# Tile loads that transpose 16-bit halves, and fifteen result tiles combined on TensorE inside the tile loop

## What is computed

```python
h = layernorm(x).reshape(-1, 256)                 # 2048 tokens
scores = sigmoid(h @ gate_w.T); sc = scores + gate_bias
# the best 4 of 8 groups, in them the best 8 of 32 experts, weights normalised, times 2.5
combine = (one_hot(tki, 32) * tkw[..., None]).sum(1)
g = silu(einsum('th,eih->tei', h, w_gate)); u = einsum('th,eih->tei', h, w_up)   # i = 128
routed = einsum('tei,ehi->th', g * u * combine[:, :, None], w_down)
shared = silu(h @ sh_gate.T) * (h @ sh_up.T) @ sh_down.T
return x + routed + shared
```

## Time and profile before

| | |
|---|---|
| median of 3 runs | 613.6 us |
| the profiled execution | 612.29 us, of which span 611.0 us |
| PE busy | 563.9 us (92%) |
| DVE busy | 407.4 us (67%) |
| ACT busy | 372.3 us (61%) |
| POOL busy | 361.8 us (59%) |
| granted clock of PE, mean | 0.976 |
| DMA | 119.69 MB, mean 196 GB/s |

### The profile page before, as it was taken

The page is one execution under the profiler, slowest core; times in us unless marked ns, Lnnn a source line. Parts: engine busy times, 40 slices in busy tenths (PEclk is TensorE's granted clock), DMA queues, the critical chain, the costliest instruction groups (busy, mean ns, idle before and its releaser), DMA issues.

```text
span 611.0 us, 11524 instructions
## 1 busy us (share of the span) xinstructions
PE 563.9 (92%) x2677; PEld 422.3 (69%) x2677; DVE 407.4 (67%) x1554; ACT 372.3 (61%) x993; POOL 361.8 (59%) x414
## 2 busy tenths in 40 slices
PE   3989989889999798798997999999999999999996
PEld 2666557655766455555666888888788888888875
DVE  6975675986768987647776444444444444688897
ACT  1867888868786755552611666566566666677760
POOL 4343233632143377876777777777777777777730
PEclk9979999999999899899799999999999999999999
DMA  8999300000000023239364999876666666999966
GB/s 258 394 397 383 131 0 2 1 1 0 2 0 0 17 92 119 98 119 343 119 222 167 304 321 342 293 223 214 200 202 205 209 207 198 346 412 407 411 255 222
DMA packets 62063, 119.69 MB, mean 196 GB/s; under 512 B 8667, under 2 KB 45583, under 8 KB 59951
## 3 DMA queue, kind: packets, MB, share of 16 engines
q1 hardware_dynamic: 48079, 77.63, 37.5%
q0 software_dynamic: 13488, 41.04, 17.7%
q10 hardware_dynamic: 432, 0.29, 0.3%
HBM read 61.29 MB, written 57.64 MB: 195 GB/s over the span
## 4 chain that ended last, share of the span: by engine, by line
PE 78%; DVE 10%; ACT 6%; DMA 3%; issue 1%; POOL 1%; SPq 0%; DVEq 0%; POOLq 0%; ACTq 0%
PE ps L2023 22%; PE ps L2043 11%; PE ps L1671 7%; PE ps L1656 6%; PE ps L1882 5%; PE ps L1682 5%; PE ps L1695 5%; PE ps L2036 3%; PE ps L1642 3%; PE ps L1777 3%; PE ps L1783 2%; DVE tokrow L750 2%; PE ps L1794 2%; DMA arena<-yrows 2%; DMA xs<-in_x 1%
## 5 line engine op out<-in xcount | busy, mean ns | idle before, releaser
L2023 PE MATMUL ps<-arena,mats 128*128 x636 | 164.0, 381 | 0.3 <-issue 0.3
L609 POOL DMA_INDIRECT xrows<-tokrow,place_of x128 | 125.2, 978 | 41.8 <-issue 37.5
L1267 DVE TENSOR_TENSOR mats<-ps,mats 128x128 f32<-128x128 f32 x159 | 46.3, 291 | 106.1 <-ACT mats L1453 101.1
L2023 PEld LDWEIGHTS ps<-arena,mats 128*128 128x128 f32 x636 | 108.6, 191 | 8.8 <-issue 0.5
L2043 PE MATMUL ps<-arena,mats 128*128 x318 | 95.5, 383 | 1.0 <-DVE mats L1274 1.0
L1453 ACT ACTIVATE mats<-ps 128x128 f32<-128x128 f32 x159 | 44.1, 277 | 56.4 <-PE ps L2023 56.4
L1446 ACT COPY mats<-ps 128x256 f32<-128x256 f32 x159 | 58.0, 365 | 11.9 <-PE ps L1882 11.9
L1387 ACT ACTIVATE hat<-tokrow,total 128x256 f32<-128x256 f32 x96 | 47.6, 499 | 18.8 <-DVE tokrow L815 11.7
L1395 ACT ACTIVATE hat<-tokrow,shift,rstd 128x256 f32<-128x256 f32 x96 | 49.7, 591 | 12.9 <-POOL shift L540 12.8
L2043 PEld LDWEIGHTS ps<-arena,mats 128*128 128x128 f32 x318 | 48.0, 191 | 13.7 <-issue 2.1
L545 POOL TENSOR_SCALAR var_eps<-variance 128x4 f32<-128x4 f32 x24 | 6.4, 269 | 83.5 <-ACT hat L1387 83.2
(11 more groups left out here) (237 smaller groups left out, 1136.0 us busy)
## 6 DMA issues: line engine op xcount, KB each, us to landing
hat<-xrows SPq DMA_DIRECT2D x81, 160.0 KB
rows<-xrows SPq DMA_DIRECT2D x78, 160.0 KB
arena<-in_experts SPq DMA_DIRECT2D x4, 1920.0 KB, 18.8
xrows<-padrow SPq DMA_DIRECT2D x32, 160.0 KB
hat<-yrows SPq DMA_DIRECT2D x5, 1024.0 KB, 8.4
tokrow<-yrows SPq DMA_DIRECT2D x5, 1024.0 KB
hatT<-yrows SPq DMA_DIRECT2D x5, 1024.0 KB, 8.9
xrows<-padrow SPq DMA_DIRECT2D x1, 4960.0 KB
```

Source lines behind the costliest of these rows:

```text
L609: gp.indirect_dma_start(out=xrows[:, :], out_offset=bass.IndirectOffsetOnAxis(ap=place_of[:, g, k:k + 1], axis=0), in_=tokrow[:, g, :], in ...
L2023: mm = te.matmul(bank(6 + u)[:, 0:2 * I], turned_row[u][:, dc * P:(dc + 1) * P], arena[:, dc * D:(E - 1) * WCOL + (dc + 1) * D][:, bass.ds ...
```

## The change

1. **Transposing loads.** `turn_row` is gone. The row buffer is filled by two DMAs on SP's queue: `dma_start_transpose` of the 256 channels seen as 512 16-bit halves, and a plain load of the 64 columns of weights and destinations. Its source needs the low halves and the high halves of a row apart, so ACT's new `halve(i)` writes them so into `slots`, one copy of 2048 halves per partition for each block; `normalise(i, 6)` now writes into `hat`, and POOL's `dispatch` waits for `halved` in place of `normed`. `copy_row` on ACT puts the halves together again: 512 halves per partition from SBUF in place of 256 floats from PSUM.
2. **Fifteen kept tiles.** KEPT is 15, tiles 144 to 158. Their four matmuls each stand inside the tile loop on PE, five iterations behind the tile's own; POOL scatters 144 tiles instead of 153. The 0/1 matrices go round six buffers. Two token tiles share a PSUM bank.
3. **Order.** ASK_AT, SUM_AT and SHIFT_AT are new; only six loads of results are asked for inside SP's loop. `ask_back(3)` waits for 112 scattered tiles. The last load of results has no buffer of its own any more and waits for sum 12 like the others.

```diff
+HALF = mybir.dt.uint16
-KEPT = 6
+KEPT = 15
+TOKEN_SETS = 6
-SHIFT_AT = 116
+SHIFT_AT = 135
-ASK_AT = [128, 129, 133, 136, 139, 142, 145, 148, 152, 155, 158]
-SUM_AT = [120, 123, 126, 129, 132, 135, 138, 141, 145, 148, 151, 154]
+ASK_AT = [140, 141, 149, 156, 157, 158]
+SUM_AT = [133, 136, 142, 148, 149, 150, 152, 153, 155, 156, 157, 158]
...
+                if g == 3:
+                    wait_scattered(-(-(YFIRST + YBUFS + 20) // YGROUP) * YGROUP)
                 if g == EARLY_SUMS:
                     wait_scattered(TILES - KEPT)
-                if g == EARLY_SUMS + 3:
-
-                    sy.wait_ge(down_done, TILES)
-                    sy.dma_start(last_back, results[g]).then_inc(row_in[0], 16)
-                    return
                 if g >= 3:
                     sy.wait_ge(out_ready, g - 2)
...
                 if n >= ROWBUFS:
-                    sy.wait_ge(row_turned, n - ROWBUFS + 1)
+                    sy.wait_ge(row_copied, n - ROWBUFS + 1)
                     sy.wait_ge(own_ready, (n - ROWBUFS) // GROUP + 1)
-                sy.dma_start(rowbuf[n % ROWBUFS], xrows[bass.ds(at[n % 4], P), :]).then_inc(row_in[n % ROWBUFS], 16)
+                sy.dma_start_transpose(rowhalf[n % ROWBUFS], halves[bass.ds(at[n % 4], P), 0:2 * D]
+                                       ).then_inc(row_in[n % ROWBUFS], 16)
+                sy.dma_start(rowbuf[n % ROWBUFS][:, WTS:ROW], xrows[bass.ds(at[n % 4], P), WTS:ROW]
+                             ).then_inc(row_in[n % ROWBUFS], 16)
...
+            def halve(i):
+                ac.wait_ge(normed[i // Q], past(i, 2 * ROUNDS, TQ))
+                ac.copy(slots[:, set_of(i), :].bitcast(HALF).rearrange("p t (h d) -> p t h d", h=2),
+                        hat[:, set_of(i), :].bitcast(HALF).rearrange("p t (d h) -> p t h d", h=2)).then_inc(halved, 1)
...
             def copy_row(s):
                 u = s % 2
-                ac.wait_ge(row_turned, s + 1)
+                ac.wait_ge(row_in[s % ROWBUFS], 32 * (s // ROWBUFS + 1))
                 if s >= 2:
                     ac.wait_ge(gate_up_done, s - 1)
-                ac.copy(turned_row[u], bank(4 + u)[:, 0:D]).then_inc(row_copied, 1)
+                ac.copy(turned_row[u].bitcast(HALF).rearrange("p (n h) -> p h n", h=2),
+                        rowhalf[s % ROWBUFS].rearrange("p (h c) r -> p h (c r)", h=2)).then_inc(row_copied, 1)
...
+            def combine(k):
+                n = TILES - KEPT + k
+                te.wait_ge(token_known, k + 1)
+                te.wait_ge(y_ready, n + 1)
+                for t in range(TQ):
+                    mm = te.matmul(bank(4 + t // 2)[:, t % 2 * D:(t % 2 + 1) * D], of_token[k % TOKEN_SETS][:, t, :],
+                                   ybuf[y_place(n)], start=k == 0 and t % 2 == 0, stop=k == KEPT - 1 and t % 2 == 1)
+                mm.then_inc(combined, 1)
...
-            for n in range(TILES + 3):
-                if 1 <= n < TILES:
-                    turn_row(n)
+            for n in range(TILES + 5):
...
-                if n >= 3:
+                if 3 <= n <= TILES + 2:
                     down(n - 3, at[n - 3])
...
+                if TILES - KEPT + 5 <= n:
+                    combine(n - 5 - (TILES - KEPT))
```

More of the change, by code:

```diff
@@ L251, in build @@
         picked = part(mats[:, 4, :, :], GROUP * E, GROUP * 2, E)
+        halves, whole_rows = xrows.bitcast(HALF), xrows.bitcast(I32)
+        rowhalf = [buf[:, 0:D].bitcast(HALF).rearrange("p (c r) -> p c r", c=2 * DC) for buf in rowbuf]
         rowgroup = [part((hat, rows)[i // 2][:, :, :], i % 2 * GROUP * ROW, GROUP, ROW) for i in range(ROWBUFS // GROUP)]
@@ L255, in build @@
             "p (k d) -> p k d", k=TOPK), hatT[0].rearrange("p c (k d) -> p (c k) d", d=D)]
-        last_back = place(arena, 0, TOPK, D)
         of_token = [part(hatT[1][:, :, :], k * TQ * P, TQ, P) for k in range(4)]
-        of_token += [part(tokrow[:, :, :], k * TQ * P, TQ, P) for k in range(KEPT - 4)]
+        of_token += [part(tokrow[:, :, :], k * TQ * P, TQ, P) for k in range(TOKEN_SETS - 4)]
         into_token = part(mats[:, 4, :, :], GROUP * E * 3, GROUP)
@@ L312, in build @@
         row_in = [sem(f"row_in{i}") for i in range(ROWBUFS)]
[L313 removed]
+        halved, row_copied, gate_up_done, silu_done = sem("halved"), sem("row_copied"), sem("gate_up"), sem("silu_done")
         matched, picked_ready, own_ready = sem("matched"), sem("picked"), sem("own")
@@ L502, in sync_program @@
                 ask_back(g)
+                if g == T and T >= len(ASK_AT):
+                    store(0, TQ)
                 if g == EARLY_SUMS - 1:
@@ L1467, in copy_out @@
                     u = y_last(n) // YGROUP
-                    ac.wait_ge(scattered[u % YGROUPS], 16 * YGROUP * (u // YGROUPS + 1))
+                    ac.wait_ge(scattered[u % YGROUPS],
+                               16 * sum(m // YGROUP % YGROUPS == u % YGROUPS for m in range(min(YGROUP * (u + 1), TILES - KEPT))))
                 ac.wait_ge(own_ready, n // GROUP + 1)
@@ L1579, in scalar_program @@
             score_tokens(0)
+            halve(0)
             evacuate(3, 3)
@@ L1589, in scalar_program @@
             score_tokens(1)
+            halve(1)
             normalise(3, 4, slots)
@@ L1607, in scalar_program @@
             score_tokens(2)
+            halve(2)
             normalise(3, 2 * ROUNDS, xs)
@@ L1611, in scalar_program @@
             score_tokens(3)
+            halve(3)
             shared_silu(2, 1)
@@ L1871, in transpose_slots @@
                 transpose_block(i, n, hat)
-            def turn_row(s):
-                u = s % 2
-                te.wait_ge(row_in[s % ROWBUFS], 16 * (s // ROWBUFS + 1))
-                if s < 2:
-                    te.wait_ge(tables_ready, 3 * (s + 2))
-                if s >= 2:
-                    te.wait_ge(row_copied, s - 1)
-                for dc in range(DC):
-                    tr = te.transpose(bank(4 + u)[:, dc * P:(dc + 1) * P], rowbuf[s % ROWBUFS][:, dc * P:(dc + 1) * P],
-                                      ident[:, :])
-                tr.then_inc(row_turned, 1)
             turn_context()
@@ L2012, in tensor_program @@
             sum_runs(2)
-            turn_row(0)
             spread_runs(2)
@@ L2063, in tensor_program @@
                     turn_act(n - 2)
-                if n >= 3:
+                if 3 <= n <= TILES + 2:
                     down(n - 3, at[n - 3])
-            te.wait_ge(row_copied, TILES)
-            te.wait_ge(act_ready, TILES)
-            for k in range(KEPT):
-                n = TILES - KEPT + k
-                te.wait_ge(token_known, k + 1)
-                te.wait_ge(y_ready, n + 1)
-                for t in range(TQ):
-                    mm = te.matmul(bank(4 + t)[:, 0:D], of_token[k][:, t, :], ybuf[y_place(n)], start=k == 0,
-                                   stop=k == KEPT - 1)
-            mm.then_inc(combined, 1)
+                if TILES - KEPT + 5 <= n:
+                    combine(n - 5 - (TILES - KEPT))
         sync_program()
```

56 lines of the change are left out of this document (26 added, 30 removed).

## The result

| | before | after |
|---|---|---|
| median | 613.9 us (612.8 to 616.1, 4 runs) | 748.9 us (745.4 to 752.0, 4 runs) |
| span of the profiled execution | 611.0 us | 746.8 us |
| ratio | | 1.219, 95% interval 1.213 to 1.226 |

The change makes the kernel 22% slower. The forecast was 626 us with a range of 604 to 646: the sign was right, the size was wrong by 123 us, and the rival that came true ("the loads set the pace") had a chance of 0.13, of which only 0.03 for a pace over 2 us.

The account below looks back on a forecast made before the run. PE and POOL's queue were taken to bound the kernel together. Late PE and DVE work ends at 619.9; 1.6 for POOL's delay and 2 for clock give a 623.5 us span, 12.5 above 611.0: 626 us, range 604 to 646.

Parts of the forecast that it names:

- the loads set the pace: Rival on SP's queue: a tile's two loads become the bound, 645 us at 1.7 us a tile; chance 0.13.
- The transposing load: SP's two loads a tile: 1.2 us to issue if alike plain ones; engines' time 0.42 to 2.8 us.
- q: Time of a tile's two loads on SP, taken as under 1.5 us; sums are delayed from 1.57 on.
- my estimate of 5.2 us a tile: Transposing load priced as four 16-bit 128x128 blocks of 1309 ns, one after another; the end would lie at 1160 us.
- 315 + 14 + 148q: When SP reaches step 148: loop start, 14 us of padding stores, 148 tile loads; forecast start of sums there was 562.
- Period of PE: PE's tile loop without turn_row: 0.22 us less a tile, from 1.63 to 1.41 us, 35 us over 159 tiles.
- copy_row: ACT's copy of 512 halves a tile: 0.54 us, hidden under PE's period; from 0.6 us it leads the last tiles.
- The holds: copy_out waits for scatters to land at tiles 130 and 133, losing about 20 of the 27 us PE gained.
- Late PE and DVE: Loop's end: nine sums from 562 us beside PE's combining, four more behind, add_kept ending 617.5; chance 0.48.
- POOL's queue as the second bound: POOL's scatters, 1.26 us each, end near PE's end (589.6 against 594), so speeding PE alone can't move the end.
- The rival in which POOL's end moves 11.5 us: Faster rival: last scatter starts at 575.46 instead of 586.95, late work is absorbed; 606 us, range 600 to 612, chance 0.28.
- Clock: PE's clock drops after idling at the holds; 2 us added, between 0 and 3.5.

Follow-up runs that it names:

- old order: Changed kernel with one plain load for its two, six kept tiles and result loads and sums placed as before: 615.8 us against 615.0 for the kernel before.
- a kernel that issued them every 1.53 us: Changed kernel with ACT instead of SP issuing the small plain load from tile 12 on: 663.4 us against 617.7 for the kernel before.
- early places: Changed kernel with one plain load, sums and result loads a few steps earlier: 625.1 us with fifteen kept tiles, 627.5 with nine, against 615.5 before.

## Why the prediction was wrong, step by step

**The transposing load: the step that failed.** The prediction has "On SP there are two issues a tile; six plain ones took 3.69 us, so 1.2 us a tile if the transposing one is alike." It is not alike: 1.21 us and 0.20 behind it against 0.43 and 0.19, so the pair takes 2.04 us, and 2.35 with what else SP does. I had bounded the data from both sides (0.42 to 2.8 us; measured 0.84) and taken the issue, which no row showed, as equal to the nearest row, with no upper end. The value taken for q, "under 1.5 us", was argued from packets alone; it measured 2.20 us behind the padding stores and 2.35 over all. The rule that I weighed, a transposing DMA as fast as a regular one ("Advanced Engine Details and Errata", section "X-Bar Transpose (TRN2)" of the Trainium skill), agrees with the packets of 18 to 20 ns and not with the issue. The other page of the Trainium skill, "VectorE: DVE Perf Modes", section "The three transpose paths", with 1309 ns for one block of 128x128, is near to what one instruction took here, 1210 ns. But that was for four blocks, and 1190 ns for two, so my estimate of 5.2 us a tile was too high, the time not being paid by the block.

**The rival's mechanism was right, its end 21 us short.** "315 + 14 + 148q" puts step 148 of SP at 663.5 with q = (371.1 - 14) / 158 = 2.26, and SP's tile load 148 started at 660.23. "At q = 1.7 it is 581, the end 19 us later [than 626]: 645" gives by the same rule 626 + 663.5 - 562 = 727.5. Measured 748.9. The formula lets sum 3, which stands in step 148, start when SP gets to step 148. But DVE came to its own step 148 only at 680.41, 20 us behind SP, after it had waited 9.9 us and 6.2 us for the loads of results 0 and 2; and then it waited 5.4 us more for load 3, which stands behind tile load 156 in SP's program and was asked at 681.39. The sum started at 686.40, 23 us behind 663.5, and that is the missing stretch. Asking the six loads earlier gave back 7 us of it by the medians and 10 by the ratios; where the rest comes from is not tried. The chance of 0.03 for a pace over 2 us follows from the missing bound: it was the one case in which no row bounded the price of the issue.

**Period of PE.** Foretold 1.41. With the plain load the timeline of PE shows 1.50 and 1.47 us:

```profile
460.74 1.13 PE L2018 MATMUL ps<-arena,mats 128*128 x4
...
462.24 1.03 PE L2018 MATMUL ps<-arena,mats 128*128 x4
...
463.71 0.48 PE L2018 MATMUL ps<-arena,mats 128*128 x1
```

The period of both kernels over 430 to 520 us agrees with that: 180 / 3 = 60 tiles on ACT in 90 us, 1.50 us each, against 165 / 3 = 55, 1.64 us each. Taking `turn_row` away gave some 0.15 us a tile, not 0.22. Over the loop that is 24 us, not 35.

**copy_row.** Foretold 0.54 us, with 0.6 as the point from which ACT leads the last tiles. The page of the changed kernel, its group of L1450:

```profile
L1450 ACT COPY mats<-hat 128x512 uint16<-128x512 uint16 x81 | 60.9, 754 | 0.0
```

0.75 us, 40% more. The row that I leaned on the earlier trace rows was a copy of 512 floats in order out of PSUM; this one gathers interleaved halves. With 0.27 of silu and 0.47 of `copy_out` (up to tile 135 the copy of `turn_act` is on DVE) ACT has 1.49 us of work a tile, and PE is busy 89.35 of the 90 us of 430 to 520: PE and ACT are about even, and no run tells which gives the period. `halve` took 1.89 us, inside its 1.6 to 2.1.

**The holds.** Foretold: `copy_out` of tile 130 ready at 520.5, held to 534.1, and that of tile 133 held to 545.0. In the run with one plain load ACT's timeline shows one hold:

```profile
541.15 0.47 ACT L1473 ACTIVATE tokrow<-ps,mats 128x256 f32<-128x256 f32 x1 [4.68 <-DMA yrows<-tokrow,mats]
```

This is tile 130, and it waited 4.7 us: it was ready only at 536.5, because the longer period (0.09 us a tile, 12 us by tile 130) and a start of the loads 3 us later in this trace (315.0 against 311.95) had eaten half of PE's gain by then, and scatter 111, started at 534.55, had landed 6.6 us later, not 2.6. Tile 133 came at 548.0 unheld. The mechanism was right at tile 130, the second hold didn't come, and the 20 us that I had the holds swallow were 4.7, as there was less gain to swallow. POOL's queue ran 2 to 3 us later than before in the two profiled kernels with one plain load and the late or the old order (scatter 111 at 534.55 and 533.50, against 531.50); I had 1.6.

**Late PE and DVE.** Foretold 562 for the start of sum 3, 617.5 for `add_kept`'s end, 1.74 us for a tile's combining. With the plain load 568.5, 626.4 (625.06 + 1.29) and, for the sixteen matmuls of the last two tiles, 3.62 us, 1.81 a tile:

```profile
568.54 1.29 DVE L1301 TENSOR_TENSOR hat<-hat 128x512 f32<-128x512 f32 x2 [2.04 <-DMA hat<-yrows]
...
614.40 3.62 PE L2047 MATMUL ps<-shared,hatT 128*128 128x256 f32 x16
...
625.06 1.29 DVE L1330 TENSOR_TENSOR xs<-ps,xs 128x512 f32<-128x512 f32 x2
```

The kernel with the plain load took 629 where I had 626. That kernel is not the change, though, and its agreement doesn't make the forecast right. It is in part luck: PE's gain was 11 us too large in my sum, and the holds that swallow it 15 us too long. The transposing load's issue is the only missing term of a size to matter for 749.

**POOL's queue as the second bound.** "What speeds up PE alone can't move the end until POOL ends sooner too." The run with the plain load in the old order shows it. Its last scatter (152), and SP's load of results 12:

```profile
589.04 0.96 POOL L708 DMA_INDIRECT yrows<-tokrow,mats  x1 [0.40 <-ACT tokrow L1478]
...
591.49 0.32 SPq L460 DMA_DIRECT2D hat<-yrows  x1
```

PE is rid of 318 transposes, and the last scatter starts at 589.04 where it started at 586.95; the time is that of before. Its releaser is a warning: `copy_out` of that tile ended at 588.76 (588.29 + 0.47), 0.3 us ahead of the scatter, so ACT and PE came no earlier than POOL. In 520 to 612 us of this trace DVE waits for loads of results and PE for DVE, and `copy_row` takes 0.75 us here too. That POOL's queue alone holds the end is therefore not shown, only that taking 0.15 us a tile off PE doesn't move it. The rival in which POOL's end moves 11.5 us and the time with it (606) didn't come true in any run: POOL's last scatter did move, to 577.93 with fifteen kept tiles and a plain load, but the sums and the combining filled the time behind it.

**Clock.** I had 2 us for it. In the kernel with the plain load the four matmuls behind the hold took 2.07 us instead of 1.03 to 1.13, at a mean granted clock of 0.83 in 532 to 545 us (twice the time: the lower level, 1.2 GHz, after 4.3 us in which PE stood still); two tiles were slow, about 2 us. In the changed kernel PE waits all through the loop, and the granted clock is 0.91 in 430 to 520 us, where before had 1.00.

No kernel that was run beats the kernel before.

## What to carry to other kernels

When work is moved from a busy engine into a DMA, price three things and not one: the bytes, the pieces, and the instruction on the queue that issues it; where no row of the trace shows the new kind of issue, give it an upper end of its own and keep a real chance for it, above all where one engine issues all transfers of a loop. A queue engine shows in no busy column: read its share in the chain and the pitch of its timeline. And when a DMA is what is waited for while the DMA engines' share falls (0.66 to 0.58 here), look at the issuer before the transfer. The other way round, a share near one (0.96 here) is no proof that anybody waits for the engines: count the tiles that each engine gets through in the same stretch.

## What the runs showed of the hardware

- A transposing DMA of 16-bit data held SP's instruction stream 1.21 us with 512 columns and 1.19 with 256 (medians of 1211 and 1188 ns), and a plain one 0.33 to 0.44 us. A second transposing instruction a tile cost 1.28 us at the same bytes.
- The packets of its queue (243 bytes in the mean) took the DMA engines 18 to 20 ns each; a kernel that issued them every 1.53 us drove the share to 0.96 at 208 GB/s, where packets of before needed 0.66 for 204 GB/s.
- ACT took 754 ns for 512 interleaved 16-bit elements a partition and 1.89 us for 2048, both out of SBUF, where 512 floats in order out of PSUM took 0.54 us: half the bytes, 40% more time. Which of the two, the source or the order, makes the difference wasn't tried.
- On three chips the kernel before took 717, 723 and 726 us (medians), on three others 615 to 618. Its mean granted clock was 0.90 to 0.92 on the first three and 0.97 to 0.98 on the chips that took 615 to 618. The two profiles of one kernel (plain load, early places, fifteen kept tiles) differ most in 340 to 430 us: PE is busy 44.03 of 90 us on the slow chip and 89.35 on the other. The cause was not found. Ratios carried over in some pairs (1.021 and 1.015, 1.016 and 1.017) and not in others (1.034 and 1.021, 1.039 and 1.062), and the holds of the late part were not there.
